# A conv, state-space scan and attention block: the backward scans read the forward orders' u and run from the last column

## The reference, cut to what matters

```python
s0 = _local_scan(xc, WSZ, False)          # 8x8 windows, by rows
s1 = _local_scan(xc, WSZ, True)           # 8x8 windows, by columns
xs = jnp.stack([s0, s1, s0[..., ::-1], s1[..., ::-1]], axis=1)
x_dbl = jnp.einsum('bkdl,kcd->bkcl', xs, x_proj_w)
dts, bs, cs = (x_dbl[:, :, :R], x_dbl[:, :, R:R + N], x_dbl[:, :, R + N:])
delta = jax.nn.softplus(jnp.einsum('bkrl,kdr->bkdl', dts, dt_projs_w) + dt_projs_b[None, :, :, None])
# step of the scan, for every column i of the order:
dA = jnp.exp(dt_i[..., None] * A)
hst = dA * hst + (dt_i * u_i)[..., None] * b_i[:, :, None, :]
y = jnp.einsum('bkdn,bkn->bkd', hst, c_i)
```

## Time and profile before

| | |
|---|---|
| median of 3 runs | 12892.73 us (12888.64 to 12894.24) |
| the profiled execution | 12887.85 us |
| its span, first to last instruction | 12886.1 us |
| block 1, scan, block 3 (from the barriers) | 890.9, 10148.7, 1846.5 us |
| busy, of the span | DVE 87%, POOL 76%, PE 68%, ACT 55% |

### The profile page before, as it was taken

How to read it: one execution, slowest core, us unless ns; L and a number is a source line. 1 busy time by engine, 2 the same in 40 slices (tenths; PEclk the granted TensorE clock), 3 DMA queues, 4 the chain that set the end, 5 groups by cost and what they waited for, 6 DMA issues and landing times. The chain is left out here.

```text
span 12886.1 us, 117201 instructions
## 1 busy us (share of the span) xinstructions
PE 8781.3 (68%) x25368; PEld 2456.9 (19%) x25368; DVE 11234.5 (87%) x7246; ACT 7092.4 (55%) x9476; POOL 9777.7 (76%) x4212
## 2 busy tenths in 40 slices
PE   7766666666666666666666666666666666588888
PEld 2221111111111111111111111111111111122323
DVE  6759999999999999999999999999999999554544
ACT  6655555555555555555555555555555555355555
POOL 0009999999999999999999999999999999312110
PEclk9877777777777777777777777777777777788888
DMA  4557777777777777777777777777777777434241
GB/s 134 168 169 173 175 176 176 175 176 175 176 174 173 175 177 175 176 176 176 176 175 176 174 172 173 176 176 175 178 176 177 176 176 175 112 75 101 71 100 30
DMA packets 581791, 2060.60 MB, mean 160 GB/s; under 512 B 82647, under 2 KB 87543, under 8 KB 566775
## 3 DMA queue, kind: packets, MB, share of 16 engines
q1 hardware_dynamic: 581366, 2056.93, 69.7%
HBM read 1599.46 MB, written 457.18 MB: 160 GB/s over the span
## 5 line engine op out<-in xcount | busy, mean ns | idle before, releaser
L822 POOL TENSOR_TENSOR dBu<-rep,BC 128x1024 f32<-128x1024 f32 x3072 | 7155.9, 2357 | 988.5 <-DMA rep<-dd_dram 952.1
L618 PE MATMUL py<-hC,fold 128*32 128x512 f32 x12288 | 2959.7, 861 | 2593.7 <-POOL hC L829 2439.1
L667 ACT ACTIVATE pd<-rep,a_now 128x1024 f32<-128x1024 f32 x3072 | 3420.8, 1114 | 1253.4 <-DVE hC L790 1004.0
L782 DVE TENSOR_TENSOR_SCAN pd<-pd,carry,dBu 128x1024 f32<-128x1024 f32 x1536 | 3596.2, 2341 | 0.0
L829 POOL TENSOR_TENSOR hC<-h,BC 128x1024 f32<-128x1024 f32 x1024 | 2402.3, 2346 | 539.1 <-DVE h L782 492.4
L790 DVE TENSOR_TENSOR hC<-pd,BC 128x1024 f32<-128x1024 f32 x2048 | 2507.6, 1224 | 169.6 <-DVE pd L782 29.2
L782 DVE TENSOR_TENSOR_SCAN h<-pd,carry,dBu 128x1024 f32<-128x1024 f32 x768 | 1798.4, 2342 | 0.0
L679 ACT ACTIVATE carry<-pd 128x1 f32<-128x1 f32 x1536 | 262.0, 171 | 2701.8 <-DVE hC L790 2571.6
L618 PEld LDWEIGHTS py<-hC,fold 128*32 128x32 f32 x12288 | 516.5, 138 | 4811.3 <-POOL hC L829 3210.6
L782 DVE TENSOR_TENSOR_SCAN pd<-pd,dBu 128x1024 f32<-128x1024 f32 x512 | 1168.1, 2282 | 38.4 <-issue 19.3
L587 PE MATMUL pp<-xdbl,w_dt 38*96 38x512 f32 x1024 | 712.3, 830 | 490.2 <-ACT xdbl L687 487.7
(11 more groups left out here) (153 smaller groups left out, 8974.3 us busy)
## 6 DMA issues: line engine op xcount, KB each, us to landing
rep<-dd_dram SPq DMA_DIRECT2D x1024, 768.0 KB, 12.8
BC<-bc_dram SPq DMA_DIRECT2D x2048, 256.0 KB, 9.0
u_dram<-p_u SPq DMA_DIRECT2D x64, 1536.0 KB, 17.6
u<-u_dram SPq DMA_DIRECT2D x128, 768.0 KB, 5.3
dd_dram<-LG SPq DMA_DIRECT2D x256, 384.0 KB, 4.5
dd_dram<-RL SPq DMA_DIRECT2D x256, 384.0 KB, 3.0
y_dram<-y SPq DMA_DIRECT2D x256, 384.0 KB, 11.1
p_y<-y_dram SPq DMA_DIRECT2D x61, 1536.0 KB, 16.0
```

The source lines that it names most:

```text
L618: last = mm(py[32 * g:32 * g + 32, t2(t)], fold[:, :], hC[:, j % 2 * 3 + g, t2(t)], start=(j % 4 == 0), stop=(j % 4 == 3), skip_group_chec ...
L667: go(pd[:, i % 2, :], rep[:, half, 0, g, :], ACT.Exp, scale=a_now[:, i:i + 1]).then_inc(S.exped, 1)
L782: v.tensor_tensor_scan(dst, pd[:, i % 2, :], dBu[:, i % 4, :], carry[:, i:i + 1] if c else 0.0, ALU.mult, ALU.add).then_inc(S.scanned, 1)
L822: nc.gpsimd.tensor_tensor(dBu[:, i % 4, :], rep[:, half, 1, g, :], BC[:, s, 0, r, :], ALU.mult).then_inc(S.dbu, 1)
```

## The change

It has four parts.

1. Block 1 no longer makes backward copies of u: `U` has two orders, `reverse` is gone (4 copies a batch) and SP stores 4 times 1.5 MB a batch in place of 8. ACT's wait for the store of Z moves from the first evacuation into Z up to the start of the norm.
2. The scan of orders 2 and 3 reads u of orders 0 and 1, takes the chunks in falling order (`stored_at`), and scans from the last column to the first: the three row operands of the scan get a step of -1 (`turned`), and `save_state` takes column 0 (`last_of`).
3. The hardware loop runs over batches: 7 rounds of 16 written-out chunks, and the last batch's 16 written out behind it. Between the orders of a batch, the copy of the second half of y and its store are made in the next sequence's first chunk, as between any two chunks. At the end of a batch they stay where they were.
4. The additions of block 3 read both operands forwards.

```diff
-            def store_u(b, h, orders):
-                for k in orders:
-                    sp.wait_ge(u_made[k], done((b * 2 + h + 1) * (NT if k < 2 else 1)))
+            def store_u(b, h):
+                for k in range(2):
+                    sp.wait_ge(u_made[k], done((b * 2 + h + 1) * NT))
...
                 if not first:
-                    store_u(b - 1, 1, (0, 1))
+                    store_u(b - 1, 1)
                 sp.wait_ge(S.z_silu, done(b + 1))
                 sp.sem_inc(S.passed, 1)
                 sp.dma_start(a.zs[b], Z[:, :, :]).then_inc(S.z_stored, 16)
-                if not first:
-                    store_u(b - 1, 1, (2, 3))
-                store_u(b, 0, (0, 1, 2, 3))
+                store_u(b, 0)
...
-                    if j == 2 and t == 0:
-                        act.wait_ge(S.z_stored, done(b * 16))
...
                 nc.scalar.preload_act_table_set("natural_log_exp_and_others")
+                act.wait_ge(S.z_stored, done(b * 16))
                 square(b, 0)
...
-            def reverse(b, h, k):
-                dve.wait_ge(u_made[k], done((b * 2 + h + 1) * NT))
-                dve.wait_ge(u_stored[k + 2], done((b * 2 + h) * 16))
-                nc.vector.tensor_copy(U[:, k + 2, :], U[:, k, ::-1]).then_inc(u_made[k + 2], 1)
...
-                    if s in (11, 13) and not first:
-                        reverse(b - 1, 1, (s - 11) // 2)
-                    if s in (21, 23):
-                        reverse(b, 0, (s - 21) // 2)
...
+        def stored_at(bk, k, c):
+
+            return bk * NC + c if k < 2 else bk * NC + NC - 1 - c
+
+        def turned(row, k):
+
+            return row if k < 2 else row[:, ::-1]
+
+        def last_of(k):
+
+            return slice(T - 1, T) if k < 2 else slice(0, 1)
...
-            with eng.Fori(0, BK - 1) as bk:
+            with eng.Fori(0, B - 1) as b:
+                for k in range(K):
+                    for c in range(NC):
+                        body(b * K + k, k, c, NC)
+            for k in range(K):
                 for c in range(NC):
-                    body(bk, c, NC)
-            for c in range(NC):
-                body(BK - 1, c, NC - 1 - c)
+                    body(BK - K + k, k, c, NC if k < K - 1 else NC - 1 - c)
...
-                sp.dma_start(u[:, s, :, :], a.u_flat[m]).then_inc(u_loaded[s], 16)
+                sp.dma_start(u[:, s, :, :], a.u_flat[stored_at(bk - k // 2 * 2, k, c)]).then_inc(u_loaded[s], 16)
...
                 if c > 0:
-                    store_y(n - 1, 1)
+                    store_y(n - 1, 1, stored_at(bk, k, c - 1))
+                elif k > 0:
+                    store_y(n - 1, 1, stored_at(bk - 1, k - 1, NC - 1))
...
-                if c == NC - 1:
-                    store_y(n, 1)
+                if c == NC - 1 and k == K - 1:
+                    store_y(n, 1, stored_at(bk, k, c))
...
-                    if i == 2 and c > 0:
+                    if i == 2 and (c > 0 or k > 0):
                         copy_y(n - 1, 1)
...
-                if c == NC - 1:
+                if c == NC - 1 and k == K - 1:
                     copy_y(n, 1)
...
-                v.tensor_tensor_scan(dst, pd[:, i % 2, :], dBu[:, i % 4, :], carry[:, i:i + 1] if c else 0.0,
-                                     ALU.mult, ALU.add).then_inc(S.scanned, 1)
+                v.tensor_tensor_scan(turned(dst, k), turned(pd[:, i % 2, :], k), turned(dBu[:, i % 4, :], k),
+                                     carry[:, i:i + 1] if c else 0.0, ALU.mult, ALU.add).then_inc(S.scanned, 1)
...
-                v.tensor_tensor(first, first, Y[:, 2, ::-1], ALU.add).then_inc(S.y_sum02, 1)
+                v.tensor_tensor(first, first, Y[:, 2, :], ALU.add).then_inc(S.y_sum02, 1)
...
-                                                   backward(Y[:, 2, :], c), ALU.add)
+                                                   Y[:, 2, c * T:(c + 1) * T], ALU.add)
```

More of the change, by code:

```diff
@@ L158, in body @@
                 sp.dma_start(a.zs[b], Z[:, :, :]).then_inc(S.z_stored, 16)
-                if not first:
-                    store_u(b - 1, 1, (2, 3))
-                store_u(b, 0, (0, 1, 2, 3))
+                store_u(b, 0)
             load_x(0)
             batch_loop(sp, body)
-            store_u(B - 1, 1, (0, 1, 2, 3))
+            store_u(B - 1, 1)
             sp.wait_ge(S.z_stored, done(16 * B))
-            for k in range(K):
+            for k in range(2):
                 sp.wait_ge(u_stored[k], done(16 * B * 2))
@@ L389, in _ @@
             batch_loop(dve, body)
-            for k in range(2):
-                reverse(B - 1, 1, k)
 def phase_scan(nc, a):
@@ L471, in load_skip, with load_u @@
                 sp.dma_start(w_skip[:], a.w_skip[bk]).then_inc(S.skip_loaded, 16)
-            def load_u(m, s):
+            def load_u(bk, k, c, s):
+                bk, k, c = bk + (k + c // NC) // K * K - k + (k + c // NC) % K, (k + c // NC) % K, c % NC
+                m = bk * NC + c
                 sp.wait_ge(S.skipped, done((m - 1) * 2))
@@ L521, in load_rep, with store_y @@
                                  a.dd[half].rearrange("x (g d) t -> d (x g) t", g=3)).then_inc(rep_loaded[half], 16)
-            def store_y(n, half):
+            def store_y(n, half, place):
                 sp.wait_ge(S.y_made, done(n * 2 + half + 1))
                 sp.sem_inc(S.passed, 1)
-                sp.dma_start(a.y_flat[n, :, half, :], y[:, half, :]).then_inc(y_stored[half], 16)
+                sp.dma_start(a.y_flat[place, :, half, :], y[:, half, :]).then_inc(y_stored[half], 16)
             load_weights(0)
             load_skip(0)
-            load_u(0, 0)
-            load_u(1, 1)
+            load_u(0, 0, 0, 0)
+            load_u(0, 0, 1, 1)
             store_bc(0, 0)
@@ L536, in _, with body @@
             store_prep(0, 1)
-            def body(bk, c, left):
+            def body(bk, k, c, left):
                 n, s = bk * NC + c, c % 2
@@ L651, in _, with pick_a @@
             go = nc.scalar.activation
-            def pick_a(bk):
+            def pick_a(bk, k):
                 act.wait_ge(S.exped, done(bk * NC * NS))
-                act.sem_inc(S.passed, 1)
-                go(a_now[:, :], a_neg[:, bk % K, :], ACT.Identity).then_inc(S.a_picked, 1)
+                go(a_now[:, :], a_neg[:, k, :], ACT.Identity).then_inc(S.a_picked, 1)
                 act.wait_ge(S.a_picked, done(bk + 1))
@@ L728, in _ @@
             act.wait_ge(S.a_ready, done(1))
-            pick_a(0)
+            pick_a(0, 0)
             for i in range(2):
@@ L766, in delta_u, with scan @@
                 v.tensor_tensor(du[:, :], pp[0:HALF, :], u[:, s, half, :], ALU.mult).then_inc(S.du_made, 1)
-            def scan(bk, c, i):
+            def scan(bk, k, c, i):
                 half, r, g = where(i)
@@ L796, in _, with body @@
             delta_u(0, 0, 1)
-            def body(bk, c, left):
+            def body(bk, k, c, left):
                 n, s = bk * NC + c, c % 2
                 for i in range(NS):
-                    scan(bk, c, i)
+                    scan(bk, k, c, i)
                     if where(i)[2] < 2:
@@ L1420, in _ @@
         def _(pool):
-            def backward(row, c):
-                return row[:, L - (c + 1) * T:L - c * T][:, ::-1]
             def add_directions(b, h):
```

22 lines of the change are left out of this document (10 added, 12 removed).

## The result

| | before | changed |
|---|---|---|
| median | 12890.68 us (12885.97 to 12894.24, 4 runs) | 12565.88 us (12557.75 to 12572.43, 4 runs) |
| profiled execution, its span | 12887.85, 12886.1 us | 12557.75, 12555.9 us |
| block 1, scan, block 3 | 890.9, 10152.8, 1842.4 us | 772.1, 9947.5, 1836.3 us |

The ratio is 0.9747, with a 95% interval of 0.9735 to 0.976. The medians are 324.8 us apart, the profiled executions 330.1. The forecast was 289 and 12603 us, so the direction is right and the gain is larger by some 36 us. The three blocks gained 118.8, 205.3 and 6.1 us. The profiled execution of the changed kernel is the quickest of its four, 8 us under their median, and its blocks are to be read with that in mind. (The scan is counted here from SP's first load to DVE's first instruction of block 3, L1279 `p_xl`, in every kernel.)

The account below looks back on a forecast made before the run. DVE's list was taken to bound the scan, a chain of waits block 1. 170 + 86 + 5 + 28 = 289 us off 12887.85 gave 12599, adjusted to the median as 12603 us; range 12565 to 12695.

Parts of the forecast that it names:

- What bounds each block: Scan: DVE's list sets the time, DVE busy 95.5%; block 1: a chain of waits between DVE, ACT and PE.
- Merged seams, 24 x 7.1 = 170: Scan: 24 of 31 sequence ends lose DVE's wait behind ACT's late copy of y and the branch, gaining 170 us.
- The 7 remaining seams still cost 7.1 us each. I take nothing more for a body four times as long: Scan, ends of batches: 7.1 us each stays, and the longer loop body changes nothing.
- Block 1, 86 + 5 + 28 = 119: Block 1: 6 x 14.4 = 86 us from earlier norms, 4.6 from the first batch, 28 at the block's end.
- Rival C: Block 1: the next wait in the ring (Z's store, DVE's strips) takes back 86 us, giving 12689 us; chance 0.09.
- a price for Z's wait: Block 1, norm's start: up to 3.1 us delay taken as hidden in ACT's wait for PE; uncovered, 22 us.
- The scan with step -1, taken at 0: Scan: 1536 backward scans cost nothing extra, judged by backward SBUF reads; upper bound 0.77 us each, 1180 us.
- Rival D: Scan: backward scans are dearer, 12664 to 12757 us or 13783 us; chance 0.07 for slower, 0.06 for a small price.
- rival B: Scan: the seam keeps a part, as POOL may set the pace; 85 us stay, 12688 us; chance 0.10.
- Block 3, taken at 0: Block 3: forward-reading additions, with unchanged traffic and load order, gain and cost nothing.
- the remaining seams get shorter too: Scan, the 7 batch ends: a gain beyond the forecast, with no size given; chance 0.02.

Follow-up runs that it names:

- e2_copy_at_end: Changed kernel with the copy of the second half of y and its store back at the end of every sequence; 12631.31 us, ratio 0.9799.
- e4_z_wait_back: Changed kernel with ACT's wait for the store of Z back at the first evacuation into Z; 12570.37 us, ratio 0.9754.
- e10_traffic_only: Changed kernel plus the old backward stores as traffic from a spare row, awaited only by SP at block 1's end; 12613.09 us, ratio 0.9789.
- e6_stores_twice: Changed kernel storing both orders of u twice, at the old stores' places, ACT waiting for both; 12783.08 us, ratio 0.992.
- e5_copies_kept: Changed kernel with DVE still making the four backward copies a batch, into spare rows never stored; 12620.83 us, ratio 0.9793.
- e1_seams_only: Kernel before with part 3 of the change alone (loop over batches, merged seams); 12692.41 us, ratio 0.9847.
- e7_no_loop: All seams merged and the scan block written out without a hardware loop, against the changed kernel; 12446.49 us, ratio 0.9658.

## Where the prediction held, and the step that failed

*What bounds each block*: right. In the scan only DVE's idle time went; in block 1 the chain of waits got shorter than DVE's saved work (119 us against 71).

*Merged seams, 24 x 7.1 = 170*: right in mechanism, and 152.1 + 26.8 = 178.9 in size. The prediction took the copy and the branch as one cause; `e2_copy_at_end` splits them into 2.6 and 4.7. Of the 8.9 us in excess, 5.5 come from the 3 seams that lie in the last batch. That batch is now written out, and each of its sequences is shorter by another 3.1 us. Against that stands the last seam of the old loop, which had no jump back and cost less than 7.1 us.

*"The 7 remaining seams still cost 7.1 us each. I take nothing more for a body four times as long"*: this is the step that failed. In the profiled execution they cost 2183.4 - 7 x 308.05 = 27.0 us, 3.9 each, and so gave back 25.2 us. That is the largest part of the 35 us that the scan gained beyond the forecast. The sentence treated the gap behind a branch as a constant of the loop. It is not one: 4.0 us before, 1.85 and 1.28 after, 1.67 and 2.27 in `e4_z_wait_back`. It also counted seven jumps where there are six, for the last end of a batch leaves the loop; ACT's gap is gone there. And it missed that code in the loop and written out do not take the same time. I had the earlier trace rows from 28 sequences in the loop and never looked at the one behind it, where both the seam (310.6 us) and the shorter pairs could be read.

How large the miss is in an average execution stays open. The same 7 ends cost 28.7 us in `e2_copy_at_end`, 32.7 in `e10_traffic_only`, 38.7, 41.3 and 41.5 in `e6_stores_twice`, `e5_copies_kept` and `e4_z_wait_back`, and 44.6 in `e1_seams_only`, against 52.2 before. So 3.9 us each is the lowest of these seven traces and 6.4 the highest. All are below the 7.1 of the forecast and the 7.5 that these ends cost before.

The Trainium skill, "Runtime: NRT & Kernel Launch", section "Instruction fetch mechanics", has the rule that I didn't weigh: instructions are fetched ahead in sequence only, and a taken branch to a page that is not at hand waits for its fetch. It fits what the traces show: "issue" gaps of ACT of 1.0 to 4.5 us (6.8 once) behind a jump back, and none at the seams without one. No run shows the fetch itself, and the page gives no duration.

*Block 1, 86 + 5 + 28 = 119*: measured 85.4 + 3.3 + 30.1 = 118.8. `e5_copies_kept` and `e10_traffic_only` confirm the parts: the wait for the store and the copies in the batches, the traffic at the end only. The two prices of the end (9 for the copies, 26 for the traffic) make more than the 30 gained there, so they overlap. Rival C (the next wait in the ring takes the gain) is refuted, and so is a price for Z's wait by `e4_z_wait_back`.

*The scan with step -1, taken at 0*: right, 220.94 us for 96 scans in both directions. Rival D is refuted. The rule of adjacent words (the Trainium skill, "Vector Engine (DVE) Microarchitecture Reference", section "Measured stream behaviour on trn2"), read strictly for a falling row, would have added an estimated 0.69 us a scan. The trace doesn't bear that out, and the measurement decides.

*POOL* (rival B): right that it doesn't set the pace. At 304.9 us a sequence in `e7_no_loop` it works 296.9 of them, and DVE waits for `dBu` once in the block (6.5 us).

*Block 3, taken at 0*: the 6.1 us can't be put down to the change. Kernels with the same forward additions took 1835.9 to 1846.7 us there, and `e1_seams_only`, with the backward ones, 1836.6.

So 289 + 25 + 9 + 6, and 1 us at the start of the scan, make the 330 of the profiled executions. The result lies at the very low end of the range, because "the remaining seams get shorter too" was given 2 chances in 100 and no price of its own.

## What to carry to other kernels

When a stall is made of a late instruction and a branch behind it in the same list, cost the two separately. The profile before may have a place with only one of them, as here, where the last round of the hardware loop leaves without jumping back. Compare a loop's body with its written-out copy before you size anything that moves work between them: here 64 dependent pairs a sequence were 0.05 us slower each in the loop, 89 us over 28 sequences, and writing the whole scan out gained 119 us. A saved copy is worth what stands around it: 71 us of DVE work in block 1 gave 119, because the copy also waited for its own earlier store, and because its stores queued at the block's end.

## What the runs showed of the hardware that was not expected

- ACT's gap behind a taken branch differs between kernels whose code of the loop is the same line for line: 1.85 + 1.28 us in the changed kernel, 1.67 + 2.27 us in `e4_z_wait_back`, one of 4.0 to 4.3 us in `e5_copies_kept`.
- The step from a DVE scan to the product that waits for it, of 2.34 us busy: 2.38 us with constants in the waits, 2.42 in a loop, 2.46 and 2.47 when the open wait is placed last of three. That order alone cost 90 us.
- A scan with a step of -1 in all its row operands takes 2341 ns, as forwards.
